# A block stack on one core: the attention's thread of the schedule set a fifth of a period ahead, and the norms' epsilon added by GpSimd

## The reference

```python
x = x + attention_and_mlp(_layernorm(x))   # 16 heads of 16, window 128; GELU MLP 256-1024-256; norms of its own
x = x + channel_mix(_layernorm(x))         # sigmoid(xr @ W_r) * (relu(xk @ W_k)**2 @ W_v), xr, xk mix x with its previous row
x = x + state_space(_layernorm(x))         # in_proj, conv of 4 taps, silu, softplus(delta), scan over 16 states, gate, out_proj
x = x + expert(_layernorm(x))              # one of 8 expert MLPs per sequence, chosen by the mean row
```

## Time and profile before

| | |
|---|---|
| median of 3 runs | 3612.49 us (3612.3 to 3615.84) |
| the profiled execution's own time | 3620.18 us |
| its span, first to last instruction | 3618.1 us |
| mean granted TensorE clock | 0.910 |
| PE, PEld busy | 3042.8, 1885.8 us |
| DVE, ACT, POOL busy | 2583.2, 2415.5, 2786.8 us |
| moved by DMA | 736.59 MB, mean 204 GB/s |

### The profile page before, as it was taken

One profiled execution on the slowest core, in us unless ns is written; L12 is line 12 of the kernel. 1 busy time (PEld: TensorE's weight loads), 2 busy tenths in 40 slices (PEclk: granted clock), 3 DMA queues, 4 the chain that ended last, 5 costly groups with the idle time before them and its releaser, 6 DMA issues.

```text
span 3618.1 us, 58031 instructions
## 1 busy us (share of the span) xinstructions
PE 3042.8 (84%) x17392; PEld 1885.8 (52%) x17392; DVE 2583.2 (71%) x5920; ACT 2415.5 (67%) x5331; POOL 2786.8 (77%) x2583
## 2 busy tenths in 40 slices
PE   5888888897988979899898989889898998987557
PEld 3555454464655646465464646556464654644236
DVE  3356878687787868778686876878687776878870
ACT  4577767676776857677685767768576776855431
POOL 1117989898887979888897988889798888977880
PEclk9998898899999989999898989989898998988678
DMA  2017877877777877877777887778878778789981
GB/s 73 7 42 192 214 208 193 225 215 238 207 204 222 217 229 216 241 209 204 223 218 228 220 237 210 207 222 226 230 215 234 210 204 231 213 248 256 284 235 37
DMA packets 423337, 736.59 MB, mean 204 GB/s; under 512 B 53427, under 2 KB 100147, under 8 KB 423027
## 3 DMA queue, kind: packets, MB, share of 16 engines
q1 hardware_dynamic: 423026, 732.89, 72.3%
HBM read 648.84 MB, written 83.89 MB: 203 GB/s over the span
## 4 chain that ended last, share of the span: by engine, by line
PE 60%; ACT 9%; POOL 9%; DVE 9%; issue 6%; DMA 5%; SPq 2%; ACTq 0%; DVEq 0%; POOLq 0%
PE bank L466 16%; PE bank L474 9%; PE bank L589 6%; PE bank L499 6%; PE bank L736 5%; PE bank L722 5%; PE bank L511 5%; POOL u_rows L1506 4%; PE bank L670 4%; DMA u_rows<-u_dram 3%; PE bank L527 3%; POOL u_rows L1499 3%; DVE u_rows L1287 3%; ACT prob L791 2%; DMA d_rows<-delta_dram 1%
## 5 line engine op out<-in xcount | busy, mean ns | idle before, releaser
L1506 POOL TENSOR_TENSOR u_rows<-u_rows,c_rows 128x512 f32<-128x512 f32 x1024 | 1304.8, 1277 | 169.3 <-DVE state L1292 116.4
L1499 POOL TENSOR_TENSOR u_rows<-u_rows,b_rows 128x512 f32<-128x512 f32 x960 | 1225.8, 1278 | 71.8 <-DMA u_rows<-u_dram 70.8
L962 ACT ACTIVATE bank<-d_rows,a_rep 128x512 f32<-128x512 f32 x1024 | 697.7, 688 | 296.5 <-DMA d_rows<-delta_dram 150.6
L1287 DVE TENSOR_TENSOR_SCAN u_rows<-bank,state,u_rows 128x512 f32<-128x512 f32 x512 | 644.0, 1271 | 83.3 <-ACT bank L962 78.9
L1287 DVE TENSOR_TENSOR_SCAN u_rows<-bank,u_rows 128x512 f32<-128x512 f32 x512 | 622.8, 1216 | 85.0 <-ACT bank L962 81.2
L791 ACT ACTIVATE prob<-prob,neg_max 128x256 f32<-128x256 f32 x1024 | 509.9, 505 | 42.9 <-DVE neg_max L1074 42.7
L670 PE MATMUL bank<-u_rows,sum_n 128*32 128x512 f32 x2048 | 309.1, 679 | 237.9 <-POOL u_rows L1506 235.0
L1074 DVE CUSTOM_DVE_ANT_0 prob<-bank,band 128x256 f32<-128x256 f32 x896 | 337.6, 416 | 178.0 <-PE bank L499 159.8
L511 PE MATMUL bank<-ident,prob 128*128 128x128 f32 x2048 | 330.3, 290 | 89.0 <-ACT prob L791 70.8
L511 PEld LDWEIGHTS bank<-ident,prob 128*128 128x128 f32 x2048 | 247.0, 148 | 230.8 <-issue 185.1
L499 PE MATMUL bank<-kT,q_own 32*128 32x256 f32 x2048 | 299.9, 412 | 47.4 <-DVE neg_max L1074 25.1
(11 more groups left out here) (167 smaller groups left out, 5276.4 us busy)
## 6 DMA issues: line engine op xcount, KB each, us to landing
u_rows<-u_dram SPq DMA_DIRECT2D x1024, 256.0 KB, 5.4
d_rows<-delta_dram SPq DMA_DIRECT2D x1024, 256.0 KB, 5.1
w<-in_W SPq DMA_DIRECT2D x28, 1024.0 KB, 7.2
zs_dram<-region_b SPq DMA_DIRECT2D x64, 256.0 KB, 2.8
xc_dram<-region_b SPq DMA_DIRECT2D x64, 256.0 KB, 2.5
u_dram<-region_b SPq DMA_DIRECT2D x64, 256.0 KB, 3.4
delta_dram<-region_b SPq DMA_DIRECT2D x64, 256.0 KB, 3.1
yg<-xc_dram SPq DMA_DIRECT2D x64, 256.0 KB, 4.9
```

Source lines behind the costliest of these rows:

```text
L962: e.activation(banks[at.bank][:, :], delta_of(i, k), ACT.Exp, scale=a_rep[:, j:j + 1]).then_inc(filled[at.bank], 1)
L1287: e.tensor_tensor_scan(rows, banks[at.bank][:, :], rows, state[:, k:k + 1] if i % 2 else 0.0, ALU.mult, ALU.add).then_inc(drained[at.bank], 1)
L1499: e.tensor_tensor(rows, rows, b_rows[:, :], ALU.mult).then_inc(bx_ready.sem, 1)
L1506: e.tensor_tensor(rows, rows, c_rows[:, :], ALU.mult).then_inc(hc_ready.sem, 1)
```

## The change

Three edits. First, the head-and-attention thread's positions are set 0.2 lower, from its first step to its last; every other thread stays. Second, `schedule` now makes order and banks together: it takes again and again the lowest position of all threads' next steps, but passes over a step that begins a bank's use when no bank is idle, and over a chain whose group isn't through the thread before or whose thread still has the group before (scans may overlap). Third, epsilon is added by POOL in front of its root instead of by DVE, and the semaphore `power` counts three steps for each norm instead of two.

```diff
 THREADS = (
-    (("head", "attention"), 0, 0.0, 1.0),
+    (("head", "attention"), 0, -0.2, 0.8),
...
+    def earlier(thread, i):
+
+        out = [] if THREADS[thread][0] == ("scan",) else [(thread, i - 1)]
+        if thread:
+            out.append((thread - 1, i | 1 if THREADS[thread][0] == ("fetch",) else i))
+        return out
...
+    while chains:
+        for key, chain in sorted(chains.items(), key=lambda c: c[1][0][:2]):
+            _, _, stage, i, step = chain[0]
+            shared = stage == "scan" and shared_inputs(i, batches)
+            names = begins.get((stage, shared, step), ())
+            if len(names) <= len(idle) and not any(c in chains for c in earlier(*key)):
+                break
+        else:
+            raise AssertionError("no bank is idle")
+        order.append((stage, i, step))
...
                 self.stat = sem(f"ln_stat_{name}", 3 * per)
-                self.power = sem(f"ln_rstd_{name}", 2 * per)
+                self.power = sem(f"ln_rstd_{name}", 3 * per)
...
-            e.wait_ge(*ln.power.at(i, 2 * k + 2))
+            e.wait_ge(*ln.power.at(i, 3 * k + 3))
...
             e.wait_ge(*ln.stat.at(i, 3 * k + 2))
-            e.tensor_scalar(ln.rstd[:, :], ln.mean_var[:, :, 1], EPS, None, ALU.add)
             e.tensor_scalar(ln.shift[:, :], ln.mean_var[:, :, 0], -1.0, None, ALU.mult).then_inc(ln.stat.sem, 1)
...
         def pool_rstd(e, ln, i, k):
 
+            e.wait_ge(*ln.stat.at(i, 3 * k + 2))
+            e.wait_ge(*ln.out.at(i, k))
+            e.tensor_scalar(ln.rstd[:, :], ln.mean_var[:, :, 1], EPS, None, ALU.add).then_inc(ln.power.sem, 1)
+            e.wait_ge(*ln.power.at(i, 3 * k + 1))
+            e.tensor_tensor(ln.rstd[:, :], ln.rstd[:, :], power[:, :], ALU.pow).then_inc(ln.power.sem, 1)
             e.wait_ge(*ln.stat.at(i, 3 * k + 3))
-            e.tensor_tensor(ln.rstd[:, :], ln.rstd[:, :], power[:, :], ALU.pow).then_inc(ln.power.sem, 1)
-            e.wait_ge(*ln.power.at(i, 2 * k + 1))
+            e.wait_ge(*ln.power.at(i, 3 * k + 2))
             e.tensor_tensor(ln.shift[:, :], ln.shift[:, :], ln.rstd[:, :], ALU.mult).then_inc(ln.power.sem, 1)
```

More of the change, by code:

```diff
@@ L111, in uses_of, with __init__ @@
     return []
+class Use:
+    def __init__(self, bank, n, f):
+        self.bank, self.n, self.f = bank, n, f
 def schedule(batches):
-    at = []
+    chains = {}
     for thread, (stages, lag, begin, end) in enumerate(THREADS):
@@ L119, in schedule @@
         for i in range(2 * batches):
-            spent = 0.0
+            chain, spent = [], 0.0
             for stage in stages:
[L122 to L127, removed]
+                if stage == "route" and i % 2 == 0:
+                    continue
+                which = i // 2 if stage == "route" else i
                 for step, cost in enumerate(COSTS[stage]):
-                    at.append((i + lag + begin + (end - begin) * spent / total, thread, stage, which, step))
+                    chain.append((i + lag + begin + (end - begin) * spent / total, thread, stage, which, step))
                     spent += cost
-    return [(stage, which, step) for _, _, stage, which, step in sorted(at, key=lambda s: s[:2])]
-class Use:
-    def __init__(self, bank, n, f):
-        self.bank, self.n, self.f = bank, n, f
-def banks_of(order, batches):
+            if chain:
+                chains[thread, i] = chain
     begins, ends = {}, {}
@@ L149, in banks_of @@
                 ends.setdefault((stage, shared, last), []).append(name)
[L150 to L153, removed]
+    def earlier(thread, i):
[3 more added lines that the diff above has]
+        return out
+    order, uses = [], {}
+    idle, counted, signalled = list(range(8)), [0] * 8, [0] * 8
+    while chains:
[8 more added lines that the diff above has]
+        order.append((stage, i, step))
+        for name in names:
             bank = idle.pop(0)
@@ L159, in banks_of @@
             idle.append(uses[stage, i, name].bank)
-    return uses
+        del chain[0]
+        if not chain:
+            del chains[key]
+    return order, uses
 def build_block_stack(nc, d):
@@ L185, in build_block_stack @@
     assert WINDOW == P and SEQ % G == 0 and HD == 16 and GROUPS == 2 and ED // EL == TILES and KE * 16 == TILES
-    order = schedule(BATCH)
-    uses = banks_of(order, BATCH)
+    order, uses = schedule(BATCH)
     with ExitStack() as ctx:
```

## The result

The changed kernel takes 3706.66 us (median of 5 runs, 3703.2 to 3718.75) against 3612.49: 1.026 times the time of before, 95% interval 1.0242 to 1.0279, +94 us. The forecast was 3564.

What follows compares the result with a forecast made beforehand. No engine was full; the prediction blamed waits where all five engines meet at each period's end. Thirteen periods gaining 5.2 us (-68) plus 20 for the two ends gave -48 on 3612.49: 3564 us, own range 3528 to 3600.

Steps and rivals of the forecast that it cites:

- the last fifth: Last of five stretches of PE's program per period: attention's end leaves it, 50.2 us becomes 42.5.
- the first fifth: First stretch of a period: PE work rises from 34.05 to 40.5 us, qkv products fill a wait; 39.7 becomes 40.0.
- the stop: Period's end: PE stands 9.20 us for POOL, itself held 8.78 us at L1440 by attention; claimed to lose its cause.
- The clock's gift of up to 3.4 us: First fifth: part of 9.07 us of matmuls at granted clock 0.62 would run at full clock, at most 3.4 us back.
- no change: Rival: the stop goes, but PE's first and POOL's fourth fifth take the gain back; 3612 us, chance 0.08.
- The price of the two ends: Timeline's start and end: 25 us more for attention's head running alone, 5 back at the end, together +20 us.
- The fourth fifth: Fourth stretch of a period: PE loses 6 us, POOL gets L1440, L1443 and norm operations; 39.2 becomes 41.5 us.
- the mark at 5 us: Sign of being wrong: in the fourth fifth, PE's output product newly waits over 5 us a period for POOL's aT.
- The second and third: Second and third stretches of a period: 15 us of attention's PE work swapped for 15; 43.5 and 38.5 us.
- the stop stays: Rival: the middle stage's delta store and reload on full queues holds the last fifth at 50; 3678 us, chance 0.20.
- Epsilon: Norms: 96 additions move from DVE to POOL; effect taken as 0, range -20 to +20 us.
- the port rule: DVE and POOL exclusively hold a shared port pair, so L1045 inherits L1044's wait; about +4 us, 3568 instead of 3564.

Runs made afterwards that it cites:

- e1: Changed kernel with the attention thread back at 0.0 and 1.0, so only epsilon is moved to POOL: 3628.78 us, 1.004 of the kernel before.
- e3: Changed kernel without the two 1 MB reloads of MLP weights and the wait for them: 3612.85 us, 0.9993 of the kernel before.
- e4: Kernel before without the two reloads of MLP weights and their wait: 3569.2 us, ratio 0.9869.
- g1: Kernel before with the MLP weight reloads parted, w_1 three steps earlier and w_2 nine steps into the MLP: 3563.55 us, 0.9859.
- g2: Changed kernel with the MLP weight reloads parted and POOL's last division ahead of its two large additions: 3587.82 us, 0.9916 of the kernel before.
- g3: Kernel before with the MLP weight reloads parted and POOL's last division ahead of its two large additions: 3557.61 us, ratio 0.9837.
- h3: Changed kernel with reloads parted and division first, the shift let in over the first four groups: 3598.21 us, 0.9941 of the kernel before.
- f1: Kernel before with the attention thread at -0.05 and 0.95: 3618.79 us, ratio 1.000.
- f2: Kernel before with the attention thread at -0.1 and 0.9: 3687.67 us, ratio 1.0196.
- f3: Changed kernel with POOL's last division ahead of its two large additions instead of between them: 3678.63 us, 1.0184 of the kernel before.
- h2: Kernel before with a shift of 0.1 and the MLP weight reloads parted: 3621.26 us, ratio 1.000.

## Why the prediction was wrong, step by step

*Right.* The scheduler costs nothing: e1 has the old order, and its period is 0.4 us longer than before, with epsilon moved. The attention's chain was what made the last fifth long, and it went: the wait of the addition of x_in (L1440) for PE is gone, PE's wait for L1506 fell from 12.7 to 1.1 us a period (9.9 us over the nine), the fifth fell from 49.8 to 44.0 (42.5 forecast).

*The step that failed: the first fifth, "the wait of 4.73 us stands in this fifth's neighbourhood and now has qkv products to fill it. I take 40.0".* It lasted 45.2 in the mean: +5.2 us a period, half of the difference between the forecast and the measured period (206.0, 216.6). The cover is there but 3.7 us long, and what it was to cover grew: the wait for nb is 6.3 us a period, not under 2, because PE waits for ACT, ACT for delta rows, and these for 2 MB of weights issued ahead of them. With the stop gone PE is at the MLP's transposes 2.1 us sooner after the weights' issue (5.6 us instead of 7.7), and the MLP's first product comes 2.5 us later after it (17.0 instead of 14.5): the rows land no sooner. e3 (-94 us for the changed kernel) shows it, e4 (-45 for before) that a smaller part of it was there already, and g1 and g2 that it goes as well when the loads are only parted. I had the row, a DMA share of 1.07, and used it for a rival only, as if transfers were either the bound of the last fifth or nothing. They were the next bound, behind the stop, in the first fifth. The clock's gift of up to 3.4 us failed with it: the granted clock was 0.92 in the changed kernel's first fifth, with the gap of 6.4 us in it, and 1.00 in e3's, without it.

*The gain that was not there.* With the crowd and the division mended the changed kernel's period is 207.0 us (g2), near the 206.0 forecast. But the same two edits bring the kernel before to 206.5 (g3), so the shift itself gains nothing a period, where -5.2 us were forecast: the 5.4 us that the last fifth gives are taken back by the other four. That is the mechanism of the rival "no change", that fuller fifths take back what the stop leaves, on which the prediction put 0.08.

*The price of the two ends.* +20 us priced, +35 measured, at period 4. I took 25 us for the head alone and 5 back at the end. The trace shows period 1 begin 22 us later (146 us, 124 before), near the 25, but the next three add 13 more, and period 15, 5 us shorter, is offset behind it. h3 corrects the picture besides: it isn't that the head runs alone, since letting the shift in gradually gives nothing back. The start of period 4 moved by 7 us for a shift of 0.05 (f1), 24 for 0.1 (f2) and 35 for 0.2, where these parts of a period are 10.5, 21 and 42 us.

*The fourth fifth.* 41.5 forecast, 42.0 measured, for a reason that I gave half: POOL is the fuller engine there (40.14 of 43.10 us), and PE, in its order, waits for POOL's last division, 4.9 us a period; half of that wait is the addition that stands before the division (f3), though taking it away made the fifth only 1.1 us shorter. The prediction named this wait among what would make it wrong, without pricing it, and set the mark at 5 us.

*The second and third.* "The same" was 1.6 and 0.7 us off; in the third 40.4 against a forecast of 38.5. Waits of PE for ACT's exponentials rose (L527, 40.4 us over nine periods; 29.7 before, L511). No run takes these apart.

The sum with measured sizes: 35 at the start, 11 x 5.8 = 64, nothing at the end: 99 us of span. The rival "the stop stays" came nearest to the result (3678) by a wrong mechanism: the stop went, and another stood behind it. It had the right suspect, the full queues, for the wrong fifth.

*Epsilon.* 0 was taken, e1 shows +14 us at the old place: inside the -20 to +20, and more than the +4 of the port rule. The rule of the Trainium skill (SBUF — State Buffer, "SBUF: two separate sides"), that the pair of ports is held for a whole instruction, told the right direction: the wait passed from L1044 to its neighbour, 471 to 599 ns. That it is the ports it waits for, no trace here shows.

## What to carry to other kernels

A stop that all engines share at one place often hides a second one; before pricing its removal, ask of each transfer and each queue there when it would be ready if nobody had stood still, and give the new time by the latest of them. Transfers that nobody needs soon are best issued away from a place where the DMA engines are full: here two loads moved by a few steps were worth 1.4%, and the order of the threads could pay only after that. Shifting a stage of a software pipeline has a fixed price at filling, which grew with the shift here (7, 24 and 35 us), so small shifts are the ones to try first: 0.05 with the other two edits gave 2.3%, where those two without it gave 1.6% (g3) and with 0.2 gave 0.8% (g2). The way between is not smooth: at 0.1 two chains fell on each other, and the time was that of the kernel before (h2).

## What was not expected of the hardware

Loads of 256 KB that land in about 5 us took 10 us with 2 MB issued ahead of them, at 337 GB/s over those 20 us, and 6.0 us at the same place without the 2 MB (e3). Moving the 2 MB a few steps to either side was enough: POOL's waits for rows are 4.4 us a period in g2 (39.5 over nine), 11.2 in the changed kernel. A small operation of DVE on 4 columns (L1060) took 599, 759 and 189 ns in the mean in the three sets of norms of e1, and 356, 976 and 637 ns in the changed kernel, while the same form took 0.15 us at its shortest before; moving its neighbour to POOL did not make it cheaper, but dearer.
